# One block for constants, queries and the first cross attention of a two-layer perceiver kernel

## The reference

```
q = layernorm(x) @ Wq + bq          # 1024 x 512, 16 heads of 32
k, v = ctx @ Wk + bk, ctx @ Wv + bv # per batch 1601 x 512 each
x = x + (softmax(q k.T / sqrt(32)) v) @ Wo + bo
```

## Time and profile before

| | |
|---|---|
| runs | 1828.0, 1828.08, 1828.59 us; median 1828.08 |
| the profiled execution | 1828.46 us, of which the span from first to last instruction is 1826.7 us |
| mean granted TensorE clock | 0.946 of full |
| PE busy | 1605.7 us (88%) |
| DVE, ACT, POOL busy | 1173.5, 914.9, 803.4 us |

### The profile page before, as it was taken

How to read it: one execution, slowest core, us unless ns; L and a number is a source line. 1 busy time by engine, 2 the same in 40 slices (tenths; PEclk the granted TensorE clock), 3 DMA queues, 4 the chain that set the end, 5 groups by cost and what they waited for, 6 DMA issues and landing times. The chain is left out here.

```text
span 1826.7 us, 34146 instructions
## 1 busy us (share of the span) xinstructions
PE 1605.7 (88%) x13913; PEld 834.3 (46%) x14024; DVE 1173.5 (64%) x1983; ACT 914.9 (50%) x1261; POOL 803.4 (44%) x402
## 2 busy tenths in 40 slices
PE   4799999999999999984889899899889989699349
PEld 2345555555555555543446453354334444344124
DVE  4478888888888888873455467788312221626881
ACT  1178778877887878774173133311112222228750
POOL 2258888888888878864008424422000000003310
PEclk9899999999999999995899889999899999799769
DMA  3469999999999999998317532243829942000001
GB/s 112 116 134 190 189 198 188 190 192 193 193 193 194 194 190 194 189 168 145 106 39 229 186 142 64 73 139 112 339 88 391 390 184 91 0 1 1 0 1 47
DMA packets 517544, 273.31 MB, mean 150 GB/s; under 512 B 443777, under 2 KB 495489, under 8 KB 514321
## 3 DMA queue, kind: packets, MB, share of 16 engines
q1 hardware_dynamic: 517392, 271.18, 61.7%
HBM read 138.74 MB, written 22.54 MB: 88 GB/s over the span
## 5 line engine op out<-in xcount | busy, mean ns | idle before, releaser
L516 POOL TENSOR_TENSOR x<-x_prob,x 128x1604 bf16<-128x1604 f32 x128 | 413.8, 3232 | 162.0 <-ACT x L647 162.0
L740 DVE TENSOR_REDUCE x_negmax<-x_score 128x1 f32<-128x1604 f32 x128 | 233.7, 1826 | 22.7 <-PE x_score L557 12.6
L540 PE MATMUL x_ring<-x_ctx_hi,wk_split 128*128 128x400 bf16 (+1 forms) x1024 | 218.3, 335 | 9.5 <-POOL x_ctx_lo L489 9.3
L629 ACT ACTIVATE x_prob<-x_score,x_negmax 128x1604 f32<-128x1604 f32 x128 | 204.8, 1600 | 23.6 <-DVE x_negmax L740 18.8
L540 PE MATMUL x_ring<-wv_split,x_ctx_hi 128*128 128x512 bf16 (+1 forms) x770 | 200.3, 379 | 9.7 <-issue 7.0
L647 ACT CAST x<-x_prob 128x1604 bf16<-128x1604 f32 x128 | 195.2, 1525 | 0.2
L704 DVE SCALAR_TENSOR_TENSOR x_kT<-x_ring,bk,x_kT 128x400 bf16<-128x400 f32 (+1 forms) x256 | 162.3, 634 | 37.6 <-ACT x_kT L618 29.9
L710 DVE TENSOR_TENSOR x_v<-x_ring,x_v 128x512 bf16<-128x512 f32 (+1 forms) x208 | 143.7, 691 | 52.5 <-ACT x_v L622 49.7
L618 ACT ACTIVATE x_kT<-x_ring,bk 128x400 bf16<-128x400 f32 (+1 forms) x196 | 116.1, 592 | 83.4 <-PE x_ring L540 82.7
L573 PE MATMUL x_pv<-x_pT,x_v 128*64 128x128 bf16 (+1 forms) x3328 | 123.2, 227 | 29.5 <-DMA x_pT<-x 20.4
L540 PEld LDWEIGHTS x_ring<-x_ctx_hi,wk_split 128*128 128x128 bf16 x1024 | 94.2, 97 | 98.0 <-issue 20.7
(11 more groups left out here) (317 smaller groups left out, 2541.5 us busy)
## 6 DMA issues: line engine op xcount, KB each, us to landing
y_ctx<-in_ctx SPq DMA_DIRECT2D x16, 1664.0 KB, 10.4
y_ctxT<-in_ctxT SPq DMA_DIRECT2D x16, 1601.0 KB, 13.9
x_stage<-in_ctxT SPq DMA_DIRECT2D x48, 400.0 KB, 4.3
x_q_rows<-q_rows SPq DMA_DIRECT2D x64, 128.0 KB, 3.4
m_xT<-in_L_ffn_w SPq DMA_DIRECT2D x16, 512.0 KB, 4.5
ffn_w_parts<-m_xT SPq DMA_DIRECT2D x32, 256.0 KB, 2.6
x_stage<-in_ctxT SPq DMA_DIRECT2D x16, 401.0 KB, 4.7
x_pT<-x SPq DMA_TRANSPOSE x256, 4.4
```

What stands on the lines that cost most here:

```text
L516: pool.tensor_tensor(ph[:, g % 2, 1, 0:NKP], prob[:, g % 2, :], ph[:, g % 2, 0, 0:NKP], ALU.subtract).then_inc(pl_done, 1)
L540: last = pe.matmul(out_, lhs, rhs, start=(i == 0), stop=(i == len(steps) - 1))
L629: nc.scalar.activation(prob[:, g % 2, :].rearrange("p (c n) -> p c n", n=QW), scores, ACT.Exp, bias=nmax[:, g % 2:g % 2 + 1], accum_out=rs ...
L740: dve.tensor_reduce(nmax[:, pair % 2:pair % 2 + 1], scores, mybir.AxisListType.XY, ALU.max, negate=True).then_inc(max_done, 1)
```

## The change

Blocks 1, 2 and 3 are gone as blocks; their instructions stand at the head of block 4. The tiles of the query stage lie in buffers that block 4 needs only later: `x` (which is also `xhat`) and `Wq` in `v` of the second batch, `xT` and the raw `Wk` in `kT` of the second batch, the raw `Wv`, the query results, `bq` and the norm's small tiles in `prob`, `picks` in `pT`. The four banks of the query stage are the four banks of `score`. The chunk loads stand ahead of the query write, and the four `split_chunk` of the first batch stand between DVE's steps of query groups 2 to 5. The wide memsets of `chi` and `clo` are now six of one key each.

```diff
-def constants(k, ident, tri, low):
-...
-def cross0_queries(k, ident, qT, wk, wv, bk):
-...
-def cross0_batches(k, ident, qT, wk, wv, bk, catT, bvT, wo):
+def cross0_batches(k, ident, tri, low, qT, wk, wv, bk, catT, bvT, wo):
...
+        x = late_v[:, 0:NT * D].rearrange("p (t n) -> p t n", t=NT)
+        wq = late_v[:, NT * D:NT * D + KD * D].rearrange("p (j n) -> p j n", j=KD)
+        xT = late_k[:, 0:KD * TOK].rearrange("p (j n) -> p j n", j=KD)
...
+        quarter = [score[:, 512 * n:512 * n + 512] for n in range(4)]
+        norm = Norm(k, ctx, "q0", x, ident, quarter[0:2], xT, lambda t: (s_x[t // 4], 16), xhat=x, home=norm_home)
...
+            for n in range(2):
+                sp.dma_start(x[:, 4 * n:4 * n + 4, :], xv[:, 4 * n:4 * n + 4, :]).then_inc(s_x[n], 16)
+            sp.dma_start(wkf, ...).then_inc(s_wkv, 16)
+            sp.dma_start(wvf, ...).then_inc(s_wkv, 16)
+            sp.dma_start(bk[:], ...).then_inc(s_wkv, 16)
+            sp.dma_start(wq, ...).then_inc(s_w, 16)
+            sp.dma_start(bq, ...).then_inc(s_w, 16)
             load_chunk(0, 0, None)
             load_chunk(0, 1, None)
+            sp.dma_start(bvT[:], d["L0_xattn_bv"]).then_inc(bv_in, 16)
+            sp.wait_ge(s_pick, 4)
+            sp.dma_start(k.picks, picks.rearrange("p h n -> p (h n)")).then_inc(s_kept, 16)
+            load_chunk(0, 2, 1)
+            load_chunk(0, 3, 2)
+            sp.wait_ge(s_kept, 16)
+            sp.wait_ge(s_qlo, len(qgroups))
             for a in range(4):
                 sp.dma_start(k.queries[:, :, 512 * a:512 * a + 512]...).then_inc(spilled, 16)
-            load_chunk(0, 2, 1)
-            load_chunk(0, 3, 2)
             sp.wait_ge(spilled, 64)
...
         @block.gpsimd
-            pool.memset(chi[:, :, QW - 1:NKP], 0.0).then_inc(set_done, 1)
-            pool.memset(clo[:, :, QW - 1:NKP], 0.0).then_inc(set_done, 1)
+            pool.memset(ident[:], 0.0).then_inc(s_const, 1)
+            pool.wait_ge(s_const, 1)
+            pool.affine_select(out=ident[:], ...).then_inc(s_ident, 1)
+            for c in range(1, 4):
+                pad = slice(QW * c + QW - 1, QW * c + QW)
+                pool.memset(chi[:, :, pad], 0.0).then_inc(set_done, 1)
+                pool.memset(clo[:, :, pad], 0.0).then_inc(set_done, 1)
             pool.memset(zero[:], 0.0).then_inc(set_done, 1)
...
         @block.tensor
+            pe.wait_ge(s_ident, 1)
+            norm.on_tensor(pe)
+            pe.wait_ge(s_w, 32)
+            pe.wait_ge(norm.s_xT, NT)
+            for n, (m, c) in enumerate(qgroups):
+                if n >= 2:
+                    pe.wait_ge(s_qf, n - 1)
+                for j in range(KD):
+                    last = pe.matmul(quarter[2 + n % 2], wq[:, j, m * P:(m + 1) * P], xT[:, j, 512 * c:512 * c + 512],
+                                     start=(j == 0), stop=(j == KD - 1))
+                last.then_inc(s_q, 1)
+            pe.wait_ge(s_split, 4)
             for n in range(NPROJ):
                 project(n, 0, n)
...
         @block.scalar
+            norm.on_scalar(nc, act)
+            act.wait_ge(s_wkv, 48)
+            act.wait_ge(bv_in, 16)
...
         @block.vector
+            norm.on_vector(dve)
+            dve.wait_ge(s_ident, 1)
             dve.tensor_tensor(fold[:], half[:, :, 0, :], half[:, :, 1, :], ALU.add).then_inc(fold_set, 1)
...
+            dve.wait_ge(set_done, 7)
+            for n, (m, c) in enumerate(qgroups):
...
+                dve.tensor_tensor(rows[:, :, 1, :], part, rows[:, :, 0, :], ALU.subtract).then_inc(s_qlo, 1)
+                if 2 <= n < 6:
+                    split_chunk(0, n - 2)
             for c in range(1, 4):
                 dve.memset(score[:, 512 * c + QW - 1:512 * c + QW], FAR).then_inc(set_pad, 1)
             dve.wait_ge(set_pad, 3)
-            split_chunk(0, 0)
-            split_chunk(0, 1)
             for n in range(NPROJ):
-                if n in (4, 11):
-                    split_chunk(0, 2 if n == 4 else 3)
                 project_lo(n, 0, n)
```

More of the change, by code:

```diff
@@ L91, with __init__ @@
 class Norm:
-    def __init__(self, k, ctx, name, x, ident, banks, xT, loaded=None, xhat=None, split=None):
+    def __init__(self, k, ctx, name, x, ident, banks, xT, loaded=None, xhat=None, split=None, home=None):
         self.split = split
@@ L387, in cross0_batches @@
         pv = k.ps(ctx, "x0_pv", [P, 512])
+        s_x = [k.sem(ctx, f"q0_x_in{n}") for n in range(2)]
+        s_w = k.sem(ctx, "q0_w_in")
+        s_wkv = k.sem(ctx, "q0_wkv_in")
+        bv_in = k.sem(ctx, "q0_bv_in")
+        s_const = k.sem(ctx, "q0_constants")
+        s_ident = k.sem(ctx, "q0_ident")
+        s_split = k.sem(ctx, "q0_split")
+        s_pick = k.sem(ctx, "q0_picks_set")
+        s_kept = k.sem(ctx, "q0_picks_kept")
+        s_q = k.sem(ctx, "q0_q_done")
+        s_qf = k.sem(ctx, "q0_qf_done")
+        s_qhi = k.sem(ctx, "q0_hi_done")
+        s_qlo = k.sem(ctx, "q0_lo_done")
+        quarter = [score[:, 512 * n:512 * n + 512] for n in range(4)]
+        norm = Norm(k, ctx, "q0", x, ident, quarter[0:2], xT, lambda t: (s_x[t // 4], 16), xhat=x, home=norm_home)
+        qgroups = [(m, c) for m in range(KD) for c in range(TOK // 512)]
         ctx_in = [k.sem(ctx, f"x0_ctx_in{n}") for n in range(2)]
@@ new lines, in _ @@
+            for c in range(1, 4):
+                pad = slice(QW * c + QW - 1, QW * c + QW)
+                pool.memset(chi[:, :, pad], 0.0).then_inc(set_done, 1)
+                pool.memset(clo[:, :, pad], 0.0).then_inc(set_done, 1)
+            pool.memset(zero[:], 0.0).then_inc(set_done, 1)
+            pool.memset(picks, 0.0).then_inc(s_pick, 1)
+            for n in range(3):
+                pool.wait_ge(s_pick, n + 1)
+                pool.affine_select(out=picks, in_=picks, compare_op=ALU.not_equal, fill=1.0, base=-32 * n,
+                                   pattern=[[-1, H], [0, P]], channel_multiplier=1).then_inc(s_pick, 1)
@@ new lines, in _ @@
+            pool.memset(tri[:], 1.0).then_inc(s_const, 1)
+            pool.memset(low[:], 0.0).then_inc(s_const, 1)
+            pool.wait_ge(s_const, 3)
+            pool.affine_select(out=tri[:], in_=tri[:], compare_op=ALU.is_ge, fill=0.0, base=0,
+                               pattern=[[1, P]], channel_multiplier=-1).then_inc(s_const, 1)
+            pool.wait_ge(s_const, 4)
+            pool.affine_select(out=tri[:, L:P], in_=tri[:, L:P], compare_op=ALU.is_ge, fill=0.0, base=-L,
+                               pattern=[[0, P - L]], channel_multiplier=1).then_inc(s_const, 1)
@@ L478, in high_part @@
+            pool.affine_select(out=low[:], in_=low[:], compare_op=ALU.is_ge, fill=FAR, base=0,
+                               pattern=[[-1, P]], channel_multiplier=1).then_inc(s_const, 1)
+            pool.wait_ge(s_const, 6)
+            pool.affine_select(out=low[:, 0:L], in_=low[:, 0:L], compare_op=ALU.is_ge, fill=FAR, base=L - 1,
+                               pattern=[[0, L]], channel_multiplier=-1).then_inc(s_const, 1)
+            pool.wait_ge(set_done, 7)
             def high_part(b, c, ready):
@@ L727, in _ @@
             dve.wait_ge(set_pad, 3)
-            dve.wait_ge(set_done, 3)
-            split_chunk(0, 0)
-            split_chunk(0, 1)
             for n in range(NPROJ):
-                if n in (4, 11):
-                    split_chunk(0, 2 if n == 4 else 3)
                 project_lo(n, 0, n)
@@ L2295, in _, with cross0 @@
                                          ALU.add).then_inc(s_x, 1)
-def cross0(k, ident, x):
+def cross0(k, ident, tri, low, x):
     d = k.d
@@ L2307, in cross0 @@
         bk = k.sb(c0, "bk", [P, NROW * KD])
-        load_small(k, [(bvT, d["L0_xattn_bv"])])
-        cross0_queries(k, ident, qT, wk, wv, bk)
         wo = k.sb(c0, "wo", [P, 4, D])
-        cross0_batches(k, ident, qT, wk, wv, bk, catT, bvT, wo)
+        cross0_batches(k, ident, tri, low, qT, wk, wv, bk, catT, bvT, wo)
         cross0_output(k, x, catT, wo)
@@ L2320, in build @@
         low = k.sb(ctx, "low", [P, P])
-        constants(k, ident, tri, low)
         x = k.sb(ctx, "x", [P, NT, D])
@@ L2324, in build @@
         k.stats = k.sb(ctx, "x_stats", [P, NT, 6])
-        cross0(k, ident, x)
+        cross0(k, ident, tri, low, x)
         state_space(k, ident, tri, x)
```

48 lines of the change are left out of this document (43 added, 5 removed).

## The result

The changed kernel takes 1811.39 us against 1828.09 before (medians of four runs each): a ratio of 0.9906, 95% interval 0.9892 to 0.9920, or 15 to 20 us. One of its four runs took 2841.33 us at a granted clock of 0.554; the median of four counts it, the ratio leaves it out. I had said 1804.5 with a range of 1801.5 to 1809.5. The direction is right and the size is not: about 7 us of the forecast 23.6 did not come. The profiled execution took 1811.17 us with a span of 1809.5, so 17.2 us of span are gone.

A forecast was written before the change was run, and what follows sets the result against it. TensorE, busy 88% of the span, was taken as the bound, with a serial chain at the start; 11.6 (start) + 9.3 (gap) + 2.7 (clock) = 23.6 us less gave 1804.5 us for the median, range 1801.5 to 1809.5.

The forecast's parts named there:

- Part 1: Program start: `x` issued at 0.79 us instead of 12.38, shifting the chain to the last query product 11.6 us earlier.
- four others: At the start: `ident`, the weight loads with `Wq`, `picks` and the load of `x` were to keep up, costing nothing.
- Rival 1: Start: POOL's wait grows under loads until `ident` is late, or the first load is slow; 1 to 5 us, chance 0.15.
- Part 2: Between query products and first projections: TensorE's 9.26 us idle go, splits fit beside the query groups at no cost.
- Rival 2: Query groups: chunk loads of 8.5 us hold DVE and stop PE for 8.7 us; 1813 us, chance 0.05.
- Part 3: First three projection groups: without the idle time before them the clock stays at 1.00, 2.7 us less.
- Rival 3: Query stage: TensorE keeps the low clock through turned tiles and products, 34.7 us more, 1839 us; chance 0.02.
- The detour of the queries: Query write and read back: ready at 72.8 us, wanted by the scores at 83.5, slack 10.7, cost 0.

The follow-up runs named there:

- e1: Changed kernel with POOL waiting for the end of VectorE's weight split before it writes `picks`; 1806.56 us, ratio 0.9877.
- e6: The kernel of e1 again, beside the unedited changed kernel on the same chip; 1806.71 us, ratio 0.9876.
- e4: Kernel before the change, with the three selects on `picks` done twice; ratio 1.0003 (0.9983 to 1.0023).
- e2: Changed kernel with POOL waiting only until rstd is computed before it writes `picks`; 1812.28 us.
- e3: Changed kernel with SP's first load of `x` waiting for `ident`; 1813.89 us in one run.
- e5: Changed kernel, unedited, run again beside the others on one chip; 1813.24 us, ratio 0.9922.
- e8: Changed kernel with the four chunk splits of the first batch put back behind the query groups; 1824.81 us.
- e7: The kernel of e1 with `x` loaded in four transfers of 0.5 MB in place of two of 1 MB; 1803.82 us, ratio 0.9863.

## Why the prediction was wrong

**The step that failed** is in Part 1: "everything on the chain from `x` to the last query product shifts by this, if four others keep up". For `picks` I asked only when POOL would be free again (18 us, wanted at 36) and not what its instructions do to VectorE, which works beside them. In the kernel before, `picks` stood beside the statistics only, which are not held; starting POOL's work and the norm at the same barrier put 8 us of memset and selects beside the chain of small operations and the first xhat. Three of the small ones and that xhat then lasted until a POOL instruction ended. The term set at nothing measured 7.4 us from the first statistics to the first turn, 0.6 of it given back in the turns. e1 and e6 take it away and get the forecast place of the first scores (83.1 and 83.3 against 83.5), with times of 1806.56 and 1806.71 us, inside the range and 2 us above the forecast; e4 brings it into the old kernel. No view of waits could have shown it, since a held operation shows as busy.

The Trainium skill, "SBUF — State Buffer", section on the two separate sides, names a pair of ports that VectorE and GpSimd share under an exclusive lock, held for a whole instruction, the loser fully blocked; VectorE contends for it in a 2-port mode, or with two inputs from SBUF when the GpSimd instruction reads SBUF too. The traces agree with the hold until a POOL instruction ends, and in the other direction with POOL as the loser (2.29 us in place of 0.29 in e2). They agree with the selection too, as far as they go: tensor-scalar operations with one tensor input are held beside the memset, which only writes, and beside selects; the tensor-tensor operations that were held stood beside selects, which read, and none stood beside the memset of `picks`, so that half of the rule is not tried here. The reciprocal (0.20 us beside a select) and the statistics (2.47 us for four beside two selects before) are not held, nor the step that reads PSUM (0.75 us in e1). The prediction weighed other pages against the trace and not this one.

**Part 1, the start.** Right: first load issued at 0.80, statistics at 6.40, 11.8 us earlier against 11.6.

**Rival 1** was half right. POOL's wait did stretch, by 4.3 us, through the loads beside it (e3). `ident` was done at 12.7 and wanted at 14.7 by e1's trace, so its slack held. Its harm was indirect, as it set where `picks` fell on the norm. With the wait of e3 (7.10 us) and `x` landing as in the changed kernel, the three selects would have run from 10.5 to 16.8, still over the small operations but clear of xhat; the chain held by them gives a first turn near 17.7 us. This is my estimate from the rows of e3 and of the changed kernel, and no run tried it, but e5 points the same way. By it the stretch is worth about 4 of the 7.1 us between 14.7 and 21.84, and the hold alone 3. Without `picks` beside the norm the stretch costs nothing: e1 has a wait of 10.07 us and its first turn at 14.71. So the rival's price, 1 to 5 us, came near by luck, for its mechanism, a late `ident` or a slow first load, did not occur.

**Part 2, the gap.** Right: the first projection follows the last product without a pause; no split waited for a chunk (each took 0.57 us at its place). Rival 2 did not occur, and its 8.7 us were too high by its own premises: it has chunk 3 asked for when the rest of chunk 2 is done, at 48.3, while Part 2 rightly has it asked for after the rest of chunk 1, at 40.8, so that 8.5 us would have landed it at 49.3 and not at 56.8. e8 shows that the barrier's removal alone would have left 4.9 of the 9.3 us idle.

**Part 3, the clock.** Right: granted clock 1.00 throughout, and 2.7 us is what e8 pays when it falls. Rival 3 did not occur: 1.00 from the first turn on, though it began 4 to 13 us earlier in these kernels.

**The detour of the queries.** Right in effect: reads issued at 70.4, 11.5 us after the write, against 12.2; chunk 0 of batch 1 was taken up at 77.71 instead of 74.3, where the shift of the earlier trace rows alone would have put it, and cost nothing.

**The sum.** The start was within 0.2 us, and so were the gap and the clock together; what POOL does to VectorE had been set at nothing without a row for it. The range failed with it, since no case in it let two engines slow each other.

## What to carry to other kernels

When work is moved so that two engines run side by side that did not before, ask of each pair what one instruction does to the other, not only when each is free; between VectorE and POOL, a 0.2 us operation can last until the 2 us instruction beside it ends, and the trace books it as busy. Put long constant work of POOL where VectorE has slack (here, under the query products), not beside a serial chain of small operations. When merging blocks, fill the seam too: a pause of 4.9 us on TensorE cost another 2.7 us at the low clock.

## What the runs showed that I had not expected

- POOL's wait before its first affine select is 7.1 to 7.2 us with quiet transfers (before, e3, e4) and 10.1 to 11.4 us with the first loads beside it.
- A 128 x 8 operation of VectorE took up to 2.30 us beside POOL, and a hold is not always one instruction long: L129 began at 12.40, 0.01 us before the `ident` select, and ended at 14.70, behind the select, the pads and the memset, which follow each other without a pause.
- The hold works in both directions: a 0.29 us select of POOL took 2.29 us beside VectorE's weight split (e2).
- TensorE's clock was at the full level at its first turn, whether that came after 13.2 us of idle time (e7) or 28.5 (e4) at the program's start, but fell within 4.9 us of idle time after work (e8).
